# Four PSUM banks for the row maxima, weighted sums without a product with zeros, and a new written-out order, in a gated cross-attention and ternary feed-forward kernel

## What is computed

```python
x = x + tanh(g_xattn[0]) * xattn(layernorm(x), ctx, ctx, mask, Wq, Wk, Wv, Wo)
x = x + tanh(g_ffn[0]) * ffn(layernorm(x), w_gate, w_up, w_down)
# x: (4, 2048, 512) fp32; ctx: (4, 77, 512); 16 heads of 32
# xattn: q = x Wq^T, k = ctx Wk^T, v = ctx Wv^T per head
#   scores = q k^T / sqrt(32), masked over the 77 keys; softmax; times v; then Wo^T
# ffn: linear(a, w) = act_quant(a) @ weight_quant(w)^T, weights ternary times a scale,
#   activations rounded to 127 steps of their row's largest magnitude
#   gate = silu(linear(x, w_gate)); up = linear(x, w_up)      (512 -> 2048)
#   out = linear(gate * up, w_down)                          (2048 -> 512)
```

## Time and profile before

| | |
|---|---|
| median of 3 runs | 1356.69 us (1356.05 to 1358.62) |
| profiled execution, its own time | 1358.6 us |
| its span, first to last instruction | 1356.8 us |
| busy in the span: TensorE, VectorE, ScalarE, GpSimd | 93%, 84%, 65%, 54% |
| mean granted TensorE clock | 0.977 of full speed |
| chain that ended last | TensorE 58%, VectorE 29%, issue 5%, DMA 3%, ScalarE 3% |

### The profile page before, as it was taken

How to read it: one execution, slowest core, us unless ns; L and a number is a source line. 1 busy time by engine, 2 the same in 40 slices (tenths; PEclk the granted TensorE clock), 3 DMA queues, 4 the chain that set the end, 5 groups by cost and what they waited for, 6 DMA issues and landing times.

```text
span 1356.8 us, 26014 instructions
## 1 busy us (share of the span) xinstructions
PE 1260.9 (93%) x7424; PEld 630.1 (46%) x7998; DVE 1144.6 (84%) x2631; ACT 878.1 (65%) x1350; POOL 735.1 (54%) x1187
## 2 busy tenths in 40 slices
PE   4776799999999999999999999999999999999996
PEld 2223444545454454545454454545445454544542
DVE  6877597898979798897979799797979989797884
ACT  5886747557584756758575665758475675847663
POOL 2113645546574664657465564756456465746662
PEclk8978899999999999999999999999999999999998
DMA  9785346574653647364564646455464736445333
GB/s 341 223 247 112 75 104 140 110 163 107 148 135 105 138 102 186 97 156 110 131 148 94 161 108 153 107 140 132 105 152 108 180 94 150 121 113 116 90 79 73
DMA packets 386793, 181.64 MB, mean 134 GB/s; under 512 B 324323, under 2 KB 357987, under 8 KB 385123
## 3 DMA queue, kind: packets, MB, share of 16 engines
q1 hardware_dynamic: 386736, 181.04, 55.1%
HBM read 61.32 MB, written 35.46 MB: 71 GB/s over the span
## 4 chain that ended last, share of the span: by engine, by line
PE 58%; DVE 29%; issue 5%; DMA 3%; ACT 3%; POOL 1%; SPq 1%; POOLq 0%; ACTq 0%; DVEq 0%
PE bank L1244 21%; PE bank L1256 15%; PE bank L1185 5%; DVE region L1046 5%; PE bank L1105 4%; DVE nmax L985 4%; PE bank L1106 3%; PE bank L1107 3%; DVE xh L975 3%; DVE xbig L1013 2%; DVE hmx L1052 2%; DVE st L1017 2%; DVE xn L970 2%; PE bank L1207 1%; PE bank L1209 1%
## 5 line engine op out<-in xcount | busy, mean ns | idle before, releaser
L628 POOL TENSOR_TENSOR region<-region,up 128x512 f32<-128x512 f32 x256 | 344.7, 1350 | 140.5 <-DVE region L1046 80.0
L1244 PE MATMUL bank<-tern_gate,region 128*128 128x512 fp8e4 x1024 | 264.8, 381 | 8.4 <-DMA region<-zb 7.3
L1244 PE MATMUL bank<-tern_up,region 128*128 128x512 fp8e4 x1024 | 263.8, 380 | 0.2 <-ACT up L781 0.2
L1256 PE MATMUL bank<-tern_down,region 128*128 128x512 fp8e4 x1024 | 234.0, 382 | 10.1 <-DMA region<-hb 9.4
L773 ACT ACTIVATE region<-bank,fs 128x512 f32<-128x512 f32 x256 | 177.4, 697 | 83.5 <-PE bank L1244 83.1
L1046 DVE SCALAR_TENSOR_TENSOR region<-region,bank 128x512 f32<-128x512 f32 x256 | 173.4, 682 | 59.9 <-ACT region L773 54.7
L1052 DVE TENSOR_REDUCE hmx<-region 128x1 f32<-128x512 f32 x256 | 170.7, 678 | 56.3 <-POOL region L628 56.2
L619 POOL TENSOR_TENSOR work<-work 124x512 f16<-124x512 f32 x160 | 191.7, 1220 | 28.7 <-ACT work L742 28.5
L582 POOL TENSOR_TENSOR rs<-mv,lnc 128x1 f32<-128x1 f32 (+1 forms) x80 | 26.7, 334 | 290.8 <-DVE mv L1020 274.0
L781 ACT ACTIVATE up<-bank 128x512 f32<-128x512 f32 x256 | 152.7, 612 | 19.6 <-PE bank L1244 18.8
L786 ACT ACTIVATE hb<-region 128x2048 bf16<-128x2048 f32 x64 | 122.7, 1918 | 56.0 <-DVE region L1068 56.0
(11 more groups left out here) (144 smaller groups left out, 2393.7 us busy)
## 6 DMA issues: line engine op xcount, KB each, us to landing
q_stack<-q_rows SPq DMA_DIRECT2D x96, 256.0 KB, 5.1
xbig<-in_x SPq DMA_DIRECT2D x16, 1024.0 KB, 5.4
q_rows<-q SPq DMA_DIRECT2D x64, 256.0 KB, 2.0
out_y<-o SPq DMA_DIRECT2D x64, 256.0 KB, 3.3
q_stack<-mT SPq DMA_DIRECT2D x32, 256.0 KB, 3.7
region<-in_wgT SPq DMA_DIRECT2D x4, 1024.0 KB, 8.3
region<-in_wuT SPq DMA_DIRECT2D x4, 1024.0 KB, 7.2
region<-in_wdT SPq DMA_DIRECT2D x4, 1024.0 KB, 5.9
```

What stands on the lines that cost most here:

```text
L628: nc.gpsimd.tensor_tensor(ht, ht, up[:, n % 2, :], ALU.mult).then_inc(hmul_ready, 1)
L1244: ins = T.matmul(pb[2 * (n % 2) + w][:, :], xqT[:, k, tok], tern[w][:, k * FF + n * GT:k * FF + (n + 1) * GT], start=(k == 0), stop=(k == ...
L1256: ins = T.matmul(pb[2][:, :], hT[:, t % 2, k, :], tern[2][:, k * GT:(k + 1) * GT], start=(k == 0), stop=(k == FK - 1))
```

## The change

- `s` uses four banks, 6, 7, 4 and 5 (`s_bank`). A product waits for the reduction four products back. The first products in banks 4 and 5 wait for the residual additions of output projection 2 and 3 of the group before (`x2_ready`), since these read the banks.
- `weighted` has no product with zeros. The chunks come in the order 0, 2, 4, 1, 3. The first product of chunk 0 carries `start=True`; the others' columns are new where no head is shared (heads 3 and 4, 6 and 7). In the odd chunks the first of the three products is split in two: the middle head alone, 33 columns, which nothing has written yet, and the two outer heads, 66 columns, which are added to. 16 products become 17. The tile of zeros and its fill are gone, and so the counts of `cast_ready` are one lower.
- The five lists of the turn are new. On TensorE: the output projection of tile 3 comes ahead of the four q chunks (it came behind); the down product 10 comes ahead of the first product for the maxima; weighted sums and score blocks of the second half alternate; weighted sum 13 comes ahead of down product 00. On VectorE: the multiplications of the first tile come ahead of their magnitudes; two normalisations and a low part of x come ahead of the output of down product 00; the scales of tile 3 (`hs30`) come behind the output of down product 20, and the split of the maxima ahead of magnitude 33. On SyncE the transposes of x stand among those of the attention output, and stores and loads of q move.

```diff
+CHUNKS = [c for c in range(0, CH, 2)] + [c for c in range(1, CH, 2)]
 TENSOR_ORDER = """
-    F:gu00 F:gu01 F:gu02 A:sc00 A:sc01 F:gu03 A:sc02 F:gu10 A:sc03 A:sc04 E:down30 A:sc10 A:sc11 A:pv00 A:pv01
-    A:sc12 F:gu11 A:sc13 A:sc14 A:pv02 A:pv03 F:gu12 F:gu13 A:pv10 A:pv11 F:gu20 A:pv12 F:down00 A:pv13 A:wo00
-    F:gu21 A:wo10 F:gu22 A:wo20 F:gu23 Q:q00 Q:q10 Q:q20 Q:q30 A:wo30 Q:s00 F:down10 Q:s01 F:gu30 Q:s10 F:gu31
-    Q:s11 F:gu32 Q:s20 F:gu33 Q:s21 Q:s30 Q:s31 F:down20 Q:mT00
+    F:gu00 F:gu01 F:gu02 A:sc00 A:sc01 F:gu03 A:sc02 F:gu10 A:sc03 A:sc04 E:down30 A:sc10 A:sc11 A:pv00 A:sc12
+    A:pv01 F:gu11 A:sc13 A:pv02 A:sc14 A:pv03 F:gu12 F:gu13 A:pv10 A:pv11 F:gu20 A:pv12 A:pv13 F:down00 A:wo00
+    F:gu21 A:wo10 A:wo20 F:gu22 F:gu23 A:wo30 Q:q00 Q:q10 Q:q20 Q:q30 F:down10 Q:s00 F:gu30 Q:s01 Q:s10 F:gu31
+    Q:s11 Q:s20 F:gu32 Q:s21 F:gu33 Q:s30 Q:s31 F:down20 Q:mT00
 SCALAR_ORDER = """
-    F:up10 A:sc10 A:sc11 A:sc12 A:ah00 F:gu11 A:ah01 F:up11 A:sc13 A:sc14 F:hb00 F:gu12 A:ah02 F:up12 F:up13
+    F:up10 A:sc10 A:sc11 A:ah00 A:sc12 A:ah01 F:gu11 F:up11 A:sc13 A:sc14 F:hb00 F:gu12 A:ah02 A:ah03 F:up12
...
 VECTOR_ORDER = """
+    E:hq30 F:gu00 F:gu01 F:gu02 F:gu03 F:hm00 F:hm01 F:hm02 F:hm03 F:hs00 E:down30 F:hq00 A:pv00 A:pv01 A:al00
+    F:gu10 A:al01 F:gu11 A:pv02 N:ln00 A:pv03 F:gu12 A:al02 A:al03 A:pv10 A:pv11 F:gu13 F:hm10 A:al10 F:hm11
+    A:pv12 N:xn00 N:xn10 A:al11 N:xl00 F:down00 A:pv13 A:al12 N:xn20 N:xl10 A:wo00 F:gu20 N:xn30 N:xl20 F:hm12
+    A:st00 A:al13 F:hm13 A:wo10 N:xl30 F:gu21 A:st10 F:hs10 F:hq10 F:hm20 A:wo20 F:gu22 A:zn00 A:za00 A:st20
+    A:wo30 A:zn10 A:st30 F:hm21 Q:q00 A:za10 F:hm22 A:zn20 Q:q10 F:gu23 A:za20 Q:q20 A:zn30 F:hm23 F:hs20 F:hq20
+    Q:q30 A:za30 Q:s00 F:down10 Q:s01 Q:s10 F:gu30 F:gu31 Q:s11 Q:s20 F:hm30 Q:s21 F:gu32 F:gu33 F:hm31 Q:s30
+    Q:s31 F:hm32 Q:mh00 F:hm33 F:down20 F:hs30
...
 SYNC_ORDER = """
+    E:tH30 A:x00 A:ta00 A:ta01 F:tH00 A:ta02 A:ta03 A:ta10 E:down30 A:ta11 N:tx00 N:tx10 A:ta12 A:kv10 N:tx20
+    A:vl00 N:tx30 A:ta13 A:vl10 Q:qd00 A:vl20 F:tH10 Q:qd10 A:tz00 Q:qs00 A:tz10 F:down00 Q:qd20 A:vl30 A:vl40
+    Q:qd30 F:tH20 Q:qs10 A:tz20 A:tz30 Q:kv00 F:down10 Q:m00 F:down20
...
+        def s_bank(g, cc):
+            return pb[cc] if early(g) else pb[(6, 7, 4, 5)[cc]]
...
             def s(g, t, half):
...
                         if cc == 0:
                             pe.wait_ge(k_max_in, g * (16 * HC) + 16 * HC)
-                    if early(g):
-                        if t:
-                            pe.wait_ge(smax_ready, g * (TT * KC) + (t * KC + cc - 3))
-                    elif t or half:
-                        pe.wait_ge(smax_ready, g * (TT * KC) + (t * KC + cc - 1))
-                    T.matmul(q_bank(g, cc)[:, 0:SROWS], q_hi[:, cc, t * P:(t + 1) * P], k_max[:, cc, :],
+                        if half and not first(g) and not early(g):
+                            pe.wait_ge(x2_ready, (g - 1) * TT + (cc + 1))
+                    else:
+                        pe.wait_ge(smax_ready, g * (TT * KC) + (t * KC + cc - 3))
+                    T.matmul(s_bank(g, cc)[:, 0:SROWS], q_hi[:, cc, t * P:(t + 1) * P], k_max[:, cc, :],
                              start=True, stop=True).then_inc(s_mm, 1)
...
-                for cc in range(CH):
+                for cc in CHUNKS:
...
-                    if cc == 0:
-                        T.matmul(bank[:, heads * HW:HH * HW], hi, v_none[:, :], start=True, stop=False)
-                    T.matmul(dst, hi, both[:, :, 0:HW], start=False, stop=False)
+                    if cc % 2 == 0:
+                        T.matmul(dst, hi, both[:, :, 0:HW], start=(cc == 0), stop=False)
+                    else:
+                        T.matmul(dst[:, 1, :], hi, both[:, 1, 0:HW], start=False, stop=False)
+                        T.matmul(dst[:, 0::2, :], hi, both[:, 0::2, 0:HW], start=False, stop=False)
                     T.matmul(dst[:, :, 0:DH], hi, both[:, :, HW:VW], start=False, stop=False)
-                    ins = T.matmul(dst, lo, both[:, :, 0:HW], start=False, stop=(cc == CH - 1))
+                    ins = T.matmul(dst, lo, both[:, :, 0:HW], start=False, stop=(cc == CHUNKS[-1]))
```

36 lines of the change are left out of this document (12 added, 24 removed).

## The result

The changed kernel takes **1344.72 us** (median of 6 runs, 1342.78 to 1347.53) against 1356.03 (1352.64 to 1358.62): ratio 0.992, 95% interval 0.9901 to 0.9939, 11.3 us less where 24.5 were forecast. The profiled execution took 1347.23 us, its span is 1345.4.

The account below looks back on a forecast made before the run. VectorE's chain was taken to bound the turn at 76.0 us, just above TensorE: 14 turns x 1.7 = 23.8, plus 0.3 and 0.4 outside, from 1358.6 to 1334.1; the median lies 1.9 lower, so 1332 us, range 1315 to 1350.

Parts of the forecast that it names:

- the fill of the zero tile goes: At the start of the run, which waits for loads anyway, the zero tile's fill disappears; no time was counted for it.
- SyncE taken as 0: Attention-output transposes sharing SyncE's queue with those of x were to cost nothing, up to 0.9 us a turn for the range.
- VectorE sets the turn at 76.3: VectorE's gapless work from down product 00 to the next turn's third gate piece keeps the turn from being under 76.3 us.
- the two blocked steps: On VectorE, a normalisation and a one-column product held up beside GpSimd, 1.54 us; four fifths kept, giving 76.0 a turn.
- TensorE's stream: TensorE alone, without its waits and with cheaper weighted sums, would need 74.45 us a turn.
- weighted pieces: Each piece of the weighted sums gains 0.055 us (up to 0.085), eight pieces a turn 0.45 us (up to 0.7).
- ScalarE's 0.5 us: In the turn's first third, ScalarE's packed queue of exponentials delays TensorE by 0.5 us (0.1 to 0.7).
- The banks: With four banks the three holes at the maxima, 1.9 us a turn, go if VectorE keeps up on average.
- the q hole: TensorE's 0.78 us wait in the projection of q goes only if VectorE reaches q0's low part in time.
- Outside the turns: Before and after the 14 turns: 0.3 us less in the front, 0.4 less for eight other weighted pieces.
- the queue wait: Rival: tile 2's transposed attention output late, or VectorE lagging at q and maxima; 0.6 to 1.5 us a turn, 1345, 17%.
- The slower case: Rival: VectorE's steps from SBUF fall more often under GpSimd's products, each full hit about 0.95 us; 1377 us, 10%.

Follow-up runs that it names:

- pad_416: Kernel after plus an unused tile of 416 bytes a partition where the tile of zeros was, no instruction changed: 1331.51 us, ratio 0.9819.
- four_ah: Kernel after with four buffers instead of two for the split attention output: 1334.71 us, ratio 0.9791.
- loads_late: Kernel after with SyncE's loads of a new batch's keys and values moved behind the transpose of half tile 13: 1343.29 us, ratio 0.9905.
- vector_less: Kernel after with VectorE taking the largest magnitude over half of the columns, part of the computation left out: 1341.14 us, one execution.
- front_zeros: Kernel after with the old weighted sums in group 0 only, tile of zeros allocated and filled again: 1329.88 us, ratio 0.9749.
- all_three: Kernel after with transpose 12 earlier, batch loads late, four attention-output buffers, and group 0's old weighted sums with the zero tile: 1321.85 us, ratio 0.9697.
- best: Kernel after with the unused 416 bytes, four attention-output buffers, transpose 12 earlier and batch loads late; new weighted sums throughout: 1325.52 us, ratio 0.9781.
- pv_only: Kernel before with the new weighted sums alone, old order and two banks for the maxima: 1381.54 us, ratio 1.0182.
- before_shifted: Kernel before with the tile of zeros allocated last, so other buffers lie as in the kernel after: 1384.41 us, ratio 1.0216.

## Why the prediction was wrong

The forecast was 1332 us; without the shift of addresses the change gives 1331.5. That is luck in part: two terms of the sum are off by some 4 us each, one either way. Of the 24.5 us forecast 13.2 are missing in the kernel after, about 7.4 in the turns and 5.7 outside.

| | forecast | kernel after | `pad_416` |
|---|---|---|---|
| normal turn | 76.0 | 76.2 | 75.35 |
| 14 turns, against 1100.8 | -23.8 | -16.4 | -28.4 |
| before the first mark and after the last, against 132.3 + 123.7 | -0.7 | +2.1 +2.9 | +1.4 +2.0 |

- **The step that failed** is "the fill of the zero tile goes": I took the tile away as work and not as an allocation. Every buffer behind it moved, the least landing time of the transposing DMAs rose by 0.1 to 0.6 us, and it costs 13.8 us (`pad_416` against its control), 12 of them in the turns. That the place of the buffers costs this much is shown; why a transpose is slower there is not. Nothing in the trace of before holds this term, but the diff does: it removes an `sb(...)` line.
- **SyncE taken as 0** is the step through which it came in. Added up from the earlier trace rows, the transposes landed within 0.3 us of need; they came later, and two holes of the output projection are 0.8 to 0.9 us a turn, my upper bound. With the old address they are 0.06. I had looked at SyncE's queue and not at ScalarE's wait for a free buffer, the longest wait of that kind in the kernel after (57.6 us, and 48.5 before), whose removal was worth 0.6 us a turn (`four_ah`).
- **The batch turns** are a case I left out: SyncE's loads stand ahead of transposes that are now needed sooner. 3.0 us in three turns (`loads_late`).
- **VectorE sets the turn at 76.3**: wrong for the kernel after. With 4.3 us less of reductions the turn fell 0.3; the agreement of 76.2 with 76.0 is a coincidence of a cause that I had at nothing with one that I had too large. One of the two blocked steps went (0.95 us), the other stayed (1.13 for 0.54), where I had kept four fifths of their time. With that put right my bound is 76.3 - 0.95 = 75.35, which is the turn of `pad_416`, and the output of down product 00 starts there 33.3 to 33.4 us after the mark, as I had it (34.0 in the kernel after). So with the old addresses the working is not contradicted, and no run took work from VectorE there. What speaks against it: of the 1.0 us of holes in that turn, those at the third gate piece and at down product 20 (0.25 and 0.39) are as large in `vector_less`, so they do not come from VectorE's load.
- **TensorE's stream** of 74.45: right (74.4). The **weighted pieces**, 0.055 each: measured 0.06 to 0.08, inside my bounds (0.6 us a turn for the 0.45), and the 33-column step is 0.02 to 0.03, as taken. The Trainium skill's floor of about 25 ns between starts, in "TensorE: Matmul & The Clock Gate", section "Wait — 56ns, not 53.3ns?", agrees with that step; the 81 ns a pair that the Trainium skill gives in the same page's "Back-to-back issue gap" still don't fit.
- **ScalarE's 0.5 us** in the first third: inside its bounds; score block 12 waits 0.06 us and weighted sum 00, which I did not name, 0.24.
- **The banks** remove 1.9 us: right in the new order, where no hole stands between products for the maxima and the q hole is gone too. But it is no term that can be added: banks alone give 0.1% (0.2% at most), the orders alone lose 2.2%, the sums alone 1.8%, and all three together gain 0.8%. Each part's worth hangs on the others, through the race of the quantisation among others. My sum was for the whole change and says nothing of the parts.
- **Outside the turns** I had -0.7 and measured +5.0. Some 0.7 and 0.9 are the address. The rest stays open. The kernels with the old weighted sums in group 0 have 5.0 and 6.1 us less there than their likes (`front_zeros` against `pad_416`, `all_three` against `best`), but each pair ran on two chips, and `four_ah`, with the new sums, has its first mark at 129.5, earlier than `front_zeros` with 130.2. Two profiles of the kernel after differ by 1.0 us at the first mark.
- **Of the rivals**, the queue wait was the one that happened (17%, around 1345), in its first form: tile 2's transposed attention output comes late, and tile 0's too. The place and the price were right, the cause was not in it. The slower case did not happen in the full change (its quantisations take 1.3 us), but its mechanism, one more step under GpSimd's product for about 0.95 us, is what made `pv_only` and `before_shifted` slow: 0.97 to 1.02 us measured.

## What to carry to other kernels

An allocation is part of a change: when a buffer goes, comes or changes size, look where the others then lie, and keep what transposing DMAs of two-byte data read and write at multiples of 256 bytes (the only remainder of three that was fast here), with an unused tile if need be. In a kernel whose TensorE and VectorE are 93% and 84% busy, one part alone cost more than the whole gained, so test the joint change and go by the holes of the trace, and look for the wait for a free buffer behind a late DMA before its place in a queue. Judge an order by who reaches a shared resource first: a lead of 0.03 to 0.044 us instead of 0.05 cost 1.1 us a turn here.

## What the runs showed of the hardware

- Transposing DMAs of two-byte data that lie at 96 or 128 modulo 256 bytes land in 4.2 and 3.0 us at least where those at 0 land in 3.6 and 2.7 (2048 and 1024 columns; with 512 columns 2.4 and 2.3), and occupy the issuing queue longer (1.69 against 1.56 us at least).
- A VectorE quantisation of 2048 columns that starts with GpSimd's product from SBUF takes 2.25 to 2.39 us instead of 1.28 if GpSimd wins, and GpSimd's product 2.36 instead of 1.27 if VectorE wins. VectorE won with a recorded lead of 0.05 us and lost with 0.044 or less.
- A hole of 4.14 us in a dense TensorE stream brought the granted clock from 1.00 to 0.50; it was back at 0.99 in 675 to 680 us.
